# Order of the tail, and two queue drains on GpSimd, in a graph attention layer

## What is computed

```python
h = jnp.maximum(_layernorm(x, axis=-1), 0.0)
s_i = h @ attn[:d]
s_j = h @ attn[d:]
e = jax.nn.leaky_relu(s_i + s_j.T, negative_slope=0.2)
e = e + jnp.where(adj > 0, 0.0, -1e9)
out = x + jax.nn.softmax(e, axis=1) @ h
```

## Time and profile before

| | |
|---|---|
| median of three runs | 815.93 us |
| the profiled execution, its time | 815.03 us |
| its span | 813.2 us |
| POOL busy | 530.5 us, 65% of the span |
| VectorE busy | 627.4 us, 77% |
| ScalarE busy | 533.9 us, 66% |
| TensorE busy | 368.4 us, 45% |
| DMA, slices 36 to 40 | 382, 48, 43, 48, 4 GB/s |

### The profile page before, as it was taken

The page is one execution under the profiler, slowest core; times in us unless marked ns, Lnnn a source line. Parts: engine busy times, 40 slices in busy tenths (PEclk is TensorE's granted clock), DMA queues, the critical chain, the costliest instruction groups (busy, mean ns, idle before and its releaser), DMA issues.

```text
span 813.2 us, 6462 instructions
## 1 busy us (share of the span) xinstructions
PE 368.4 (45%) x1380; PEld 163.5 (20%) x1380; DVE 627.4 (77%) x2101; ACT 533.9 (66%) x411; POOL 530.5 (65%) x526
## 2 busy tenths in 40 slices
PE   0554444344443444434434444344344436645652
PEld 0332111111111111111111111111111214423651
DVE  6898379777768667698768776797779899898733
ACT  4985676676766767676666666766766677677330
POOL 6630677755557777756557777676557767777771
PEclk9885655555555555555555555555555655866676
DMA  8999999999999999999999999999999999991110
GB/s 344 401 399 429 385 409 404 410 412 410 412 410 406 409 405 409 407 414 413 413 409 410 404 410 407 408 412 414 411 416 410 405 410 408 406 382 48 43 48 4
DMA packets 39719, 300.22 MB, mean 369 GB/s; under 512 B 10752, under 2 KB 17528, under 8 KB 22272
## 3 DMA queue, kind: packets, MB, share of 16 engines
q1 hardware_dynamic: 24032, 277.04, 83.7%
q0 software_dynamic: 15360, 22.51, 8.1%
q10 hardware_dynamic: 288, 0.26, 0.1%
HBM read 303.76 MB, written 8.98 MB: 385 GB/s over the span
## 4 chain that ended last, share of the span: by engine, by line
DMA 69%; issue 13%; DVE 8%; ACT 3%; PE 3%; POOL 2%; POOLq 0%; ACTq 0%; DVEq 0%
DMA adj_ring<-in_adj_dram 66%; DVE near L779 3%; ACT sign_ring L632 2%; PE words L1515 2%; DMA h_table<-sums 2%; POOL near L539 1%; DVE one_hot L748 1%; DMA near<-h_table,near_id 1%; ACT h_all L644 1%; DVE h_all L784 1%; DMA out_dram<-adj_ring 0%; DVE sums L1047 0%; DVE cand L793 0%; PE words L1511 0%; DVE terms L1042 0%
## 5 line engine op out<-in xcount | busy, mean ns | idle before, releaser
L632 ACT ACTIVATE sign_ring<-adj_ring,half_neg 128x4096 fp8e3<-128x4096 int32 x128 | 474.8, 3710 | 206.5 <-DMA adj_ring<-in_adj_dram 202.0
L539 POOL DMA_INDIRECT near<-h_table,near_id x384 | 416.8, 1085 | 207.6 <-issue 118.3
L1475 PE MATMUL words<-sign_ring,pack_w 128*128 128x512 bf16 x512 | 223.1, 587 | 349.8 <-ACT sign_ring L632 349.8
L793 DVE MAX8 cand<-words 128x8 f32<-128x256 f32 x256 | 91.0, 418 | 97.0 <-PE words L1475 97.0
L1475 PEld LDWEIGHTS words<-sign_ring,pack_w 128*128 128x128 bf16 x512 | 54.5, 126 | 515.5 <-ACT sign_ring L632 446.1
L1047 DVE TENSOR_REDUCE sums<-terms 128x128 f32<-128x1024 f32 x58 | 111.7, 1926 | 2.0
L550 POOL DMA_INDIRECT near_m<-h_table,id_m x64 | 65.1, 1016 | 19.5 <-issue 19.5
L1042 DVE TENSOR_TENSOR terms<-near,weight 128x512 f32<-128x512 f32 (+1 forms) x87 | 72.3, 857 | 0.0
L1466 PE MATMUL words<-place,place_w 128*128 128x512 bf16 x128 | 61.6, 581 | 3.3 <-DVE key L954 3.3
L1501 PEld LDWEIGHTS listing<-cand,one_hot 128*128 128x128 f32 x128 | 32.6, 312 | 11.4 <-issue 7.4
L1456 PE MATMUL listing<-h_all 128*1 128x128 f32 x128 | 20.2, 334 | 25.5 <-ACT h_all L644 25.5
(11 more groups left out here) (293 smaller groups left out, 524.5 us busy)
## 6 DMA issues: line engine op xcount, KB each, us to landing
adj_ring<-in_adj_dram SPq DMA_DIRECT2D x128, 2048.0 KB, 24.4
near<-h_table,near_id POOLq DMA_INDIRECT x384, 6.4
h_table<-h_all POOLq DMA_DIRECT2D x4, 1056.0 KB, 14.9
x_all<-in_x_dram SPq DMA_DIRECT2D x4, 1024.0 KB, 9.4
out_dram<-x_all SPq DMA_DIRECT2D x30, 128.0 KB, 23.5
near_m<-h_table,id_m POOLq DMA_INDIRECT x64
out_dram<-x_all ACTq DMA_DIRECT2D x2, 128.0 KB, 3.0
adj_ring<-h_table SPq DMA_DIRECT2D x1, 132.0 KB, 2.6
```

The costliest lines, as they stand in the source:

```text
L539: pool.indirect_dma_start(out=near[:, p % RING, k, :], out_offset=None, in_=table, in_offset=bass.IndirectOffsetOnAxis(ap=near_id[:, p % I ...
L632: nc.scalar.activation(bytes_of, adj_ring[:, n % HALVES, :].rearrange("p (d r i) -> p d r i", r=2, i=WORDS), ACT.Sign, bias=half_neg[:, :] ...
L793: last = nc.vector.max(out=cand[:, p % 2, t % 2, 8 * q:8 * q + 8], in_=words[t % 3][:, q * PART:(q + 1) * PART])
L1475: last = nc.tensor.matmul(at[:, k * BANK:(k + 1) * BANK], pack_w[:, d, :], twins[:, o + k * BANK:o + (k + 1) * BANK], start=False, stop=(d ...
```

## The change

GpSimd gets a `drain` instruction in its loop behind the gathers of pairs 28 and 29. Behind the loop, `store_lone(0)` moves behind the far loop, and `store_m(3)` goes ahead of `store_lone(1)`. On ScalarE, the register loads, the exponential and the diagonals of pair 31 go ahead of the close and store of pair 30, and `exp_lone` goes behind these. On VectorE, `lone_part` is split in its first pass (`lone_raw`) and the other two (`lone_mask`), and pair 31 is weighed between them; `lone_end(1)` goes behind `add_deep(3)`.

```diff
+        DRAINED = (PAIRS - 4, PAIRS - 3)
...
                 if p == FIRST_STEP + 2:
                     load_lone(0)
+                if p in DRAINED:
+                    nc.gpsimd.drain()
                 m = p // SEG - 1
...
             gather_m(SEGS - 1, range(0, DEEP))
             load_lone(LAST)
-            store_lone(0)
             pool.wait_ge(sizes_ready, 2)
...
+            store_lone(0)
+            store_m(SEGS - 1)
             store_lone(LAST)
-            store_m(SEGS - 1)
...
             write_diagonals(BODY + 1)
-            close_pair(BODY + 1)
-            store_pair(BODY + 1)
-            exp_pair(BODY + 2)
             act.wait_ge(sizes_ready, 2)
             tiles = act.value_load(far_tiles[0:1, 0:1], min_val=1, max_val=TILES)
             parts = act.value_load(far_parts[0:1, 0:1], min_val=1, max_val=DC)
+            exp_pair(BODY + 2)
+            write_diagonals(BODY + 2)
+            close_pair(BODY + 1)
+            store_pair(BODY + 1)
             for c in range(LONE_PARTS[LAST]):
                 exp_lone(LAST, c)
-            write_diagonals(BODY + 2)
             close_pair(BODY + 2)
...
-            def lone_part(b, c):
+            def lone_raw(b, c):
...
+            def lone_mask(b, c):
+                lt = TILES // LONE_PARTS[b]
+                form = [P, lt, LONE_CAP[b]]
+                part = lone_p[b][c % len(lone_p[b])]
+                tiled = part.rearrange("p (t e) -> p t e", e=LONE_CAP[b])
                 dve.wait_ge(lone_masking[b], 2 * c + 1)
...
                 for c in early_parts(p - FIRST_STEP):
-                    lone_part(0, c)
+                    lone_raw(0, c)
+                    lone_mask(0, c)
...
             score_pair(BODY + 2)
-            for c in range(LONE_PARTS[LAST]):
-                lone_part(LAST, c)
+            lone_raw(LAST, 0)
             weigh_pair(BODY + 2)
+            lone_mask(LAST, 0)
...
-            lone_end(LAST)
             score_deep(SEGS - 1)
             add_deep(SEGS - 1)
+            lone_end(LAST)
```

## The result

The changed kernel takes 818.65 us (median of ten runs) where the kernel before takes 814.36 beside it: a ratio of 1.0051, 95% interval 1.0036 to 1.0066. The prediction was 807 in a range from 803.5 to 817. It was wrong, and on the wrong side: I forecast a gain and measured a loss. The profiled execution has a span of 816.8 us.

A forecast was written before the change was run, and what follows sets the result against it. The prediction took DMA, nearly all the adjacency stream, as 69% of the span, with the gain in the last 100 us: span 813.2 - 4.2 (order) - 4.6 (end drain) = 804.4, forecast 807 on the median's scale, range 803.5 to 817.

The forecast's parts named there:

- I take 6.37 for the first drain and under 0.5 for the second: POOL, behind pairs 28 and 29: assumed cost in us of the two added drains.
- pair 30 starts 1 to 2.5 later than 733.96: POOL's gathers: pair 30 delayed only 1 to 2.5 us by the added drains, a 3.9 us pause taking the rest.
- Both bounds of a single drain: Cost of one POOL drain: at least 0.17 us; at most 6.37, or 5.1 behind a landing of 6.1.
- a spill of the forecast: Drains on POOL: settling starts with the landing, pair 30 about 9 late, end drain short, 812; chance 0.12 within 0.52.
- the slower rival: POOL behind pairs 28 and 29: full drain price recurs from the landing, tail 15 to 16 late, 822; chance 0.15.
- The end drain: POOL's drain at the block's end: shortened to 0.5 us behind the last landing, a gain of 4.6 us.
- 11 ns each: POOL drain upkeep: 5.1 us spread over about 466 DMAs, so 47 DMAs leave 0.5 us at the end.
- The order: Reordered tail on ScalarE, VectorE and POOL: pair 31's mix ends 3.3 us earlier, the last DMA starts 4.2 us earlier.
- The cover: Slack behind POOL's added drains: 2.8 us at score_pair(31), some 3.8 at score_deep, 3.7 at the far store; lateness covered.
- The slack counted for the far store: POOL's far store: 3.7 us of slack, 1.2 before 791.2 and 2.5 before store_m.
- the cheap drain: Rival: added drains on POOL are cheap and the end drain stays, order alone gains, 811.7; chance 0.14.
- the price that recurs in full, whatever was drained before: Rival: each POOL drain costs its 6.37 us again, 815 to 816, no change; chance 0.19.

The follow-up runs named there:

- the repeat: The changed kernel without its two drains, timed a second time against the kernel before: 809.59 us, ratio 0.9942.
- the order alone: The changed kernel without its two drains, only the new order of the tail, against the kernel before: 807.86 us, ratio 0.9931.
- the table of counts: Drain ends past the landing over all runs, including the kernel before with drains behind pairs 1, 2, 4, 7, 11, 16, 22 and twice behind 29: 809.82 us.
- the quiet place: The changed kernel with its drains moved behind pairs 30 and 31, where the matrix no longer streams: 808.76 us in one execution.

## Why the prediction was wrong

**The step that failed** is "I take 6.37 for the first drain and under 0.5 for the second", and with it "pair 30 starts 1 to 2.5 later than 733.96". Both bounds of a single drain were sound: 0.17 below, and above 5.1 behind a landing of 6.1, some 11 us after the issue. I took values that let the wait for the landing count almost nothing: in the 6.37 it is that of the last store, 1.2 us behind the record of its issue, and in the 0.5 it is left out. It counts in full. Counted as the 6.37 was, from the end of the last record ahead, drain 1 cost 9.3 us and drain 2, with 12 DMAs, 5.0; from the issue they cost 10.3 and 6.0, of which 6.1 and 5.4 are the landing under the stream. I had named this as a spill of the forecast (pair 30 about 9 late, 812) and as the slower rival (15 to 16 late, 822). Measured is 12.75 late and 818.65, between the two, nearer to the rival. The rival has drain 1 right (721.1, measured 721.4); its second drain, with the full 5.1 behind the landing, is 4.6 too dear.

**The end drain.** "11 ns each", so 47 DMAs leave 0.5 us: the line through 0 and 466 DMAs was the wrong shape. 47 cost 2.8 us, because the price is some 41 to 64 ns each for up to about 100 and no longer rises in step behind that. That the end drain shrinks was right; it gave 2.5 us instead of 4.6.

**The order.** The forecast was 4.2 us, and measured are 5.6 alone (0.0069 x 812.85), 4.7 in the repeat (0.0058 x 814.68). The mechanism was right: the diagonals of pair 31 ready before TensorE is, and all behind moves with it, up to what POOL's queue allows. The term that was too small is the mix of pair 31, for which I carried over the 6.0 to 6.2 us that the mixes took before, at a lower granted clock and, for pair 31, in step with its diagonals; it took 4.0.

**The cover.** I counted 2.8 us of slack at score_pair(31) and more behind it. Beside the order alone, pair 30 of the changed kernel is 13.4 us late (746.71 and 733.28), the last store 12.8 (811.72 and 798.96), and the span 10.2 longer (816.8 and 806.6), with 2.5 given back by the end drain. So only 0.6 of the lateness was covered, and two things took the cover away. The slack counted for the far store was gone once TensorE was faster: with the order alone that store already waits 4 us for POOL's queue, and in the changed kernel it leaves the same way, 12.4 later. And the slack at score_pair(31) rests on a landing of 2.5 us, where the last gather took 6.3. That path is the later one: the last sums are ready at 810.1, and store_m, which POOL's queue would have let go at 808.2, waits 2.55 us for them. The slower mix doesn't explain it. From score_pair(31)'s start to the last sums the changed kernel takes 26.8 us (783.34 to 810.14), the order alone 27.1 (769.70 to 796.81); the lateness is there before the mix begins.

**The two rules cited.** Drains of about 12 ns at the end of a kernel (the Trainium skill, "VectorE: DVE Perf Modes", section "The DRAIN you can't avoid") are not what POOL shows here: 52 ns directly behind another drain, 4 to 9 us at the block's end. (The rival that the prediction means by "the second" there is its third, the cheap drain.) The Trainium skill, "Perfetto Trace Analysis", section "Sequencer-only Instruction (DRAIN, etc)", says that the record starts once the instruction's semaphores are satisfied and covers its execution. The trace doesn't contradict it: the record of drain 1 starts at 695.1, 16 us ahead of the last issue at 711.11, and ends at 721.4. So it holds the time in which POOL still works through the gathers ahead, and can't be read as a price.

**The rivals.** The cheap drain is refuted by the pauses, and the price that recurs in full, whatever was drained before, by the table of counts. What recurs is the wait for the landing, which the quiet place shows best: the same 12 DMAs, 7.4 us behind a landing of 6.9 and 3.0 behind one of 2.4.

## What to carry to other kernels

Price a drain from the last issue ahead of it: the landing at that place, plus an upkeep by the DMAs since the last drain, which up to some 100 of them can be told and beyond can't. If one is worth it at all, put it where POOL waits for a landing anyway and shortly before the end, not where transfers land slowly and an unbroken queue stands behind it. When one instruction has one sample in a trace, ask which of its parts would be longer at the new place before carrying the sum over.

## What the runs showed that I had not expected

- A drain's price behind many DMAs isn't steady: 1.3 us past the landing with 414, in two runs, and 6.5 with 458.
- TensorE's fp32 mix of a pair takes 4.0 us in an unbroken run at a granted clock of 1.00, 4.9 at 1.00 in step with its diagonals, and 6.0 to 6.4 at 0.72 and 0.62 behind a pause. Why the clock fell in some pauses and not in the one of 2.65 us stays open.
- Lateness on one queue can make a transfer meet another that it used to miss: the last gather of pair 31 and the far loop's loads.
